# A two-layer transformer block on one core: routed rows without their gate row, an on-chip join at the end, new engine orders and no filler matmuls

## The chip, the cores and the metric

One core of a Trainium2 chip runs the kernel as a single program. The metric is device time in microseconds (us), the median over the runs shown. Beside it stands one profiled execution, whose trace gives the start and length of every instruction.

## What is computed

Eight sequences of 256 tokens, 256 wide, in float32, go through two layers. In each, a mixer and then a feed-forward part are added to `x` under gains `ga`, `gb` that depend on the sequence:

```python
x = x + ga * _L0_attn_ref(h, ...)     # causal attention, 16 heads, 4 kv heads
x = x + gb * _L0_ffn_ref(h, ...)      # 8 experts of width 176, top 2, and a shared one
x = x + ga * _L1_attn_ref(h, ...)     # linear attention with a memory
x = x + gb * _L1_ffn_ref(h, ...)      # 16 experts of width 256, top 4
# _L1_ffn_ref: G = gates of the top 4 (softmax), else 0
h = jnp.einsum('mh,eoh->emo', t, w1) + b1[:, None, :]
act = a * jax.nn.sigmoid(ALPHA * a) * (b + 1.0)
y = jnp.einsum('emi,edi->emd', act, w2) + b2[:, None, :]
return x + jnp.einsum('me,emd->md', G, y)
```

The change concerns the last part. Its 2048 tokens have four experts each, so 8192 (token, expert) pairs are computed, and each pair's result is scaled by its gate in `G` and by the sequence's gain row `gb` and summed into its token's row.

## The kernel before, in words

The work is cut into eight batches `b` of 256 tokens (one sequence each). For a batch, attention of layer 0 (128 units `u` of one head and one sequence, stages `scores`, `s_max`, `s_exp`, `p_t`, `pv`, `o_out`, `wo`), the first feed-forward part (`f_...`, `s_...`, `d_...`), linear attention of layer 1 (`qk_mm`, `vv_mm`, `ls_mm`, `num`, `o1`, `wo1`) and routing (`f_src` to `f_send`) follow each other, while attention of later batches goes on beside them. TensorE, VectorE (DVE), ScalarE (ACT), GpSimd (POOL) and the DMA queue of SyncE (SP) each run one fixed list of stages. `lay_out()` makes these lists before the program is built: it gives each stage a weight (`ENGINE`), a time to land (`LANDING`) and each chain of stages an allowance (`ALLOWED`, `DURING`, `BEHIND`), and always takes the chain that comes first by these numbers. An engine that waits holds up all that stands behind in its list.

**Routing.** Each batch's tokens are written to their experts' regions of a table `xsD` in DRAM. A row has `ROW` = 529 numbers: 256 of the token, its number, 16 gates and, from 273 on, the 256 numbers of the gain row `gb`, halved, which ACT puts there (`f_gb`, L1353). POOL sends the rows with eight indirect DMAs a batch (`f_send`, L1990), each of 128 rows. Earlier, SP fills the whole table with zero rows (`clear`, L820).

**Blocks.** When five batches are routed (`PART`), DVE and TensorE count the rows of each expert (`n_mm`, `n_blk`, `n_pre`, `n_tab`, `n_sel`, `n_bi`) and blocks of 128 rows begin: `FIRST` = 22 blocks from the first five batches, mixed with the rest of the other work, and then 57 more in a plain loop, 79 in all (`NBLK`). Block `n` is loaded by SP (`xb`, L851, into a ring `XB`), turned by TensorE (`x_t`, L1133), multiplied with its expert's `w1` in two halves (`h_m0`, `h_mm`, L1140), which ACT scales into `WS` (`w_in`, L1423) from `W1` (loaded in pieces by `w12`, L870, the last when the last `wo` is done), activated by DVE and ACT (`e_a` L1844, `e_tanh`, `e_b`, `e_g`, `e_act` L1864), and multiplied with `w2` (`y_mm`, L1161; `w2x`, L860). DVE multiplies the result by the gate and by the gain row (`y_out`, L1872) into one of five buffers `YB`, and POOL adds it by an indirect accumulating DMA to the tokens' rows in DRAM (`y_add`, L2019; the row numbers come from `tok`, L2009). Even blocks add to the output itself, odd ones to a second array `accD`. Two adds to one array never run together: `y_add(n)` waits for `y_add(n-2)`, and `y_out(n)` for `y_add(n-5)`, whose buffer it takes.

**Output.** POOL finishes a batch's `x` (`f_gain` L1977, `f_x` L1982), SP stores it to the output (`store`, L874), and the adds go on top. At the end one accumulating DMA adds `accD` to the output (`merge`, L2025).

**Fillers.** `FILL` names twelve stages of TensorE ahead of whose waits `fill` issues products of a constant (L900, 128x512, 35 in all) that nobody reads.

```python
def fill(*stage):
    n = FILL.get(stage, 0)
    ...
    for _ in range(n):
        pe.matmul(bank[plan.at[stage]][:, :], identb, cb16[:, 0:512], start=True, stop=True)
```

Of the kernel before, what the change touches and what calls it, by code (L numbers as in the profile page):

```python
# [15 lines left out]
NBLK, REG, ROW = 79, 2048 + 128, 529  # L16
# [3 lines left out]

PIECES, INSIDE = (range(0, 6), range(6, 11)), (range(0, 5), range(4, 8))
# [3 lines left out]
ALLOWED = {"keys": (0.04, 0.932), "query": (0, -0.52), "first": (0.1, 0.1), "shared": (0.04, 0.04), "dense": (0, -0.127), "linear": (0.08, 0.004), "late": (0.1, 0.201), "route": (0.1, 0.108), "gain": (0.1, 0.336), "count": (0.1, 0.207), "weights": (0.1, -0.153), "token": (0.2, 0.25), "unit": (0.1, 0.438), "block": (0.2, 0.2), "turn": (0.18, 0.044)}  # L25
DURING, BEHIND = {5: 0, 6: 0}, {5: -2.03, 6: 0.04, 7: 0}
# [4 lines left out]
    for name, stages in {  # L31
# [3 lines left out]
        "route_on_pe": "f_t f_gate f_rank s_mm s_t", "route_on_act": "f_sq f_src f_ht f_hb f_gb f_sig f_exp s_tanh s_at",  # L35
# [16 lines left out]
    for engine, stages in {  # L52
        "PE": "n_mm 0.25 n_pre 0.2 n_sel 0.95 x_t 0.25 h_m0 0.9 h_mm 1.07 y_mm 0.95 g_t 0.25 g_mm 0.95 h_t 0.45 k_mm 1.72 v_mm 1.72 k_t 0.45 mod_mm 1.72 modc_mm 3.6 f_t 0.47 f_gate 0.9 f_rank 0.4 s_mm 1.2 s_t 0.22 d_mm 0.3 d_t 0.42 d_y 2.15 "
              "p_t 0.33 scores 0.67 q_mm 1.73 q_t 0.45 pv 0.65 wo 0.87 qk_mm 1.73 vv_mm 0.84 ls_mm 0.65 num 0.56 o1_t 0.22 wo1 0.91",
        "ACT": "w_in 1.45 x_out 0.38 e_tanh 0.43 g_out 0.4 h_mod 1.05 k_sq 1.6 v_out 0.6 f_ht 0.62 f_hb 0.62 f_sig 0.2 f_sq 0.9 f_src 0.9 f_gb 0.6 f_exp 0.7 s_tanh 0.3 s_at 0.38 d_tanh 0.35 d_at 0.7 "
               "silu_t 0.3 gate_t 0.2 s_exp 0.99 p_tout 0.5 q_tout 0.62 p_norm 0.82 o_out 0.4 el_exp 0.64 vv_out 0.4 o1_out 0.4",
        "DVE": "n_blk 0.9 n_tab 1 n_bi 0.5 e_a 0.65 e_b 0.62 e_g 0.43 e_act 0.43 y_out 0.5 g_add 0.75 silu 0.4 b1_one 0.1 gate 0.2 zrow 0.13 ones_v 0.06 mod_out 0.7 mod_clamp 1.5 mod_one 0.3 modc_out 0.3 ln_var 1.25 ln_x 0.76 f_var 0.2 f_top 1.05 f_hot 0.75 f_gw 0.5 f_sum 0.3 f_macc 0.2 f_w 0.9 f_pos 0.95 "
# [127 lines left out]
def do(stage, *key, **how):  # L185
# [9 lines left out]
    ((("scores", NU - 1),), (11, 12), (15, 16)),  # L195
    ((("pv", NU - 1),), (13, 14)),
    ((("wo", NU - 1),), (9, 10)),
)


FILL = {
    ('num', 6, 0): 3,
    ('f_t', 0, 7): 6,
    ('h_m0', 0): 3,
    ('d_t', 7, 0, 1): 2,
    ('f_rank', 1, 6): 3,
    ('y_mm', 2): 2,
# [1875 lines left out]
```

## Time and profile before

| | |
|---|---|
| median of 3 runs | 1038.71 us (1037.44 to 1038.74) |
| profiled execution | 1032.54 us, its span 1030.5 us |
| instructions | 20559 |
| mean granted TensorE clock | 0.981 of full speed |
| TensorE busy | 976.0 us, 95% of the span |
| DVE, ACT, POOL busy | 716.3, 674.0, 427.2 us |

The page of the profile lists busy times by engine, the span in slices, the DMA queues and the costliest groups. PE is TensorE (its weight loads are PEld), SPq and POOLq are the queues of SP and POOL, and a line such as L1872 is a line of the kernel. The clock of TensorE is given as a share of 2.4 GHz. Time after `<-` says what ended the idle time before an instruction.

### The profile page before, as it was taken

What the parts mean: (1) busy time and instruction counts of PE and PEld (TensorE: products, weight loads), DVE (VectorE), ACT (ScalarE), POOL (GpSimd) and SP (SyncE); (2) the same over time, 40 slices, a digit from 0 to 9 for tenths busy, and PEclk for the clock granted to TensorE, in tenths of its full rate; (3) what the DMA queues carried; (4) which work ended last, traced back from release to release, by engine and by line L of the source; (5) the groups of instructions that cost most, each with busy time, mean ns of one, the idle gap of its engine ahead of it and who ended that gap; (6) DMA issues with size and microseconds to landing.
All of it is one profiled execution on the core that took longest, in us unless ns stands there. A gap on an engine that the chain in (4) does not pass through costs nothing. (4 is left out here: it accounts for less than half of the span.)

```text
span 1030.5 us, 20559 instructions
## 1 busy us (share of the span) xinstructions
PE 976.0 (95%) x6074; PEld 822.2 (80%) x6074; DVE 716.3 (70%) x2498; ACT 674.0 (65%) x1944; POOL 427.2 (41%) x447
## 2 busy tenths in 40 slices
PE   8999999999999999999999999998979899999980
PEld 4769878978878887888888788886758689999980
DVE  3564656766776778777768767864877678888870
ACT  2757877688668667758867867784735367777650
POOL 3322512331361254165146216331174555666662
PEclk9999999999999999999999999999999999999995
DMA  9926992998699120020021004355176799999944
GB/s 307 305 88 240 377 375 74 349 378 307 219 347 376 70 84 23 2 104 33 1 94 43 2 1 166 95 205 187 28 197 143 213 253 223 224 229 219 228 118 82
DMA packets 94108, 180.52 MB, mean 175 GB/s; under 512 B 9949, under 2 KB 29085, under 8 KB 93229
## 3 DMA queue, kind: packets, MB, share of 16 engines
q1 hardware_dynamic: 73899, 148.55, 43.6%
q0 software_dynamic: 18752, 30.30, 12.9%
q8 instruction: 48, 0.79, 0.3%
q14 instruction: 63, 0.52, 0.2%
q10 hardware_dynamic: 1346, 0.36, 0.2%
HBM read 77.71 MB, written 107.99 MB: 180 GB/s over the span
## 5 line engine op out<-in xcount | busy, mean ns | idle before, releaser
L1957 POOL TENSOR_TENSOR RB<-RB 128x512 f32<-128x512 f32 x64 | 67.0, 1047 | 262.1 <-DVE RB L1741 262.0
L1140 PE MATMUL bank<-RB 128*128 128x128 f32 x1264 | 157.3, 276 | 2.2 <-ACT RB L1423 0.8
L1140 PEld LDWEIGHTS bank<-RB 128*128 128x128 f32 x1264 | 149.6, 192 | 5.6 <-ACT RB L1423 1.8
L1106 PE MATMUL bank<-RA,RB 128*128 128x256 f32 x512 | 133.5, 383 | 4.8 <-ACT RB L1324 4.8
L1423 ACT ACTIVATE RB<-RA,nw 128x512 f32 x158 | 105.6, 716 | 43.0 <-issue 16.9
L1078 PE MATMUL bank<-RA 128*128 128x256 f32 x512 | 121.4, 380 | 1.6 <-DMA RA<-in_L_attn_Wq 1.6
L1078 PEld LDWEIGHTS bank<-RA 128*128 128x128 f32 x512 | 94.9, 190 | 17.0 <-issue 2.8
L1106 PEld LDWEIGHTS bank<-RA,RB 128*128 128x128 f32 x512 | 91.6, 191 | 18.5 <-ACT RB L1324 5.7
L1933 POOL TENSOR_TENSOR qs<-qs,half 128x4 f32<-128x4 f32 x64 | 65.7, 1026 | 62.7 <-DVE qs L1750 49.6
L1161 PE MATMUL bank<-RB,BC 128*128 128x256 f32 x316 | 83.8, 389 | 2.2 <-DVE BC L1864 1.3
L1324 ACT ACTIVATE RB<-bank 128x256 f32<-128x256 f32 x128 | 48.7, 381 | 52.0 <-PE bank L1097 47.0
L1741 DVE COPY RB<-bank 128x512 f32<-128x512 f32 x64 | 44.2, 691 | 49.0 <-PE bank L1078 48.7
L1990 POOL DMA_INDIRECT xsD<-SC,pu x64 | 65.1, 1018 | 31.1 <-DVE pu L1677 16.7
L1096 PE MATMUL bank<-RB,RA 128*128 128x256 f32 x256 | 77.4, 384 | 0.0
L1305 ACT ACTIVATE RB<-bank 128x384 f32<-128x384 f32 x128 | 62.0, 490 | 22.2 <-PE bank L1057 22.0
L1068 PE MATMUL bank<-RA 128*128 128x256 f32 x256 | 76.4, 380 | 0.0
L1298 ACT ACTIVATE RB<-RB,sm 128x128 f32<-128x128 f32 x128 | 50.8, 397 | 24.0 <-DVE sm L1762 19.6
L1318 ACT ACTIVATE RB<-RB,sm 128x256 f32<-128x256 f32 x128 | 64.0, 500 | 0.0
L1299 ACT ACTIVATE RB<-RB,sm 128x256 f32<-128x256 f32 x128 | 63.9, 499 | 0.0
L1057 PE MATMUL bank<-ident,RB 128*128 128x128 f32 x384 | 63.2, 274 | 0.0
L1161 PEld LDWEIGHTS bank<-RB,BC 128*128 128x128 f32 x316 | 55.2, 194 | 9.7 <-DVE BC L1864 2.4
L1844 DVE TENSOR_SCALAR RB<-bank,b 128x128 f32<-128x128 f32 x158 | 48.1, 346 | 21.1 <-PE bank L1140 14.4
(255 smaller groups left out, 2381.8 us busy)
## 6 DMA issues: line engine op xcount, KB each, us to landing
xsD<-BC SPq DMA_DIRECT2D x17, 4232.0 KB, 32.9
RB<-in_w2b SPq DMA_DIRECT2D x79, 256.0 KB
RB<-xsD SPq DMA_DIRECT2D x61, 264.5 KB, 3.6
BC<-modD SPq DMA_DIRECT2D x16, 512.0 KB, 4.2
RA<-in_w SPq DMA_DIRECT2D x10, 512.0 KB
X<-xsD SPq DMA_DIRECT2D x18, 264.5 KB, 3.0
RA<-in_L_attn_Wq SPq DMA_DIRECT2D x1, 2048.0 KB, 13.8
RA<-in_L_attn_Wo SPq DMA_DIRECT2D x1, 2048.0 KB, 19.7
```

The lines of the kernel that those rows point to most:

```text
L1068: pe.matmul(ps[:, 128:384], q[:, 128:256], k[:, 0:256], start=True, stop=True).then_inc(mine("scores", u), 1)
L1078: m = pe.matmul(psum("q_mm", p)[:, t * 256:t * 256 + 256], hT[:, b % 2, c, t * 128:t * 128 + 128], Wq[:, c, h * 128:h * 128 + 256], start= ...
L1096: pe.matmul(psum("pv", u)[:, 0:256], v[:, 0, :], PT[:, u % 2, 0:256], start=True, stop=False, skip_group_check=True)
L1106: m = pe.matmul(bank[5][:, t * 256:t * 256 + 256], OT[:, u % 2, t * 128:t * 128 + 128], Wo[:, h, :], start=(h == 0 and t == 0), stop=(h == ...
L1140: m = pe.matmul(ps[:, 128 * j:128 * j + 128], WS[:, n % 2, c, 128 * j:128 * j + 128], XT[:, n % 2, c * 128:c * 128 + 128], start=(c == 0), ...
L1161: m = pe.matmul(ps[:, 0:256], AB[:, n % 3, c * 128:c * 128 + 128], W2[:, n % 4, c, :], start=(c == 0), stop=(c == 1))
L1299: act.activation(P[:, u % 4, 128:384], P[:, u % 4, 128:384], ACT.Exp, bias=s[:, 3:4], scale=-1.0, accum_out=s[:, 5:6]).then_inc(mine("s_ex ...
L1318: act.activation(P[:, u % 4, 128:384], P[:, u % 4, 128:384], ACT.Copy, scale=s[:, 7:8]).then_inc(mine("p_norm", u), 1)
L1423: m = act.activation(WS[:, n % 2, c, :], W1[:, bass.ds(r, 1), c, :].rearrange("p a n -> p (a n)"), ACT.Copy, scale=nw[:, c:c + 1])
L1933: pool.tensor_tensor(dst, src, half[:, 0:n], ALU.pow).then_inc(sem, 1)
L1957: pool.tensor_tensor(sq, qrow, qrow, ALU.mult).then_inc(mine("q_sq", p), 1)
L1990: pool.indirect_dma_start(xsD[:, :], bass.IndirectOffsetOnAxis(pu[:, i, k:k + 1], 0), route(1)["src"][:, i, 0:ROW], None).then_inc(mine("f ...
```

## The change

- Rows of `xsD` shrink from 529 to 273 numbers: the gain row is gone from `clear`, `f_send` and `xb`, with the stage `f_gb` that wrote it. `y_out` multiplies by the gate and 0.5 alone.
- All adds go to two arrays of their own, `accA` and `accB`, both set to zero early on. `store` and `merge` are gone. After the last add SP loads `accA` (`sum_a`) and ACT's queue `accB` (`sum_b`), 256 KB each for a batch; `join` adds the two, multiplies by the gain rows (`gains`, loaded in the loop) and adds `x`, for batches 2 and 5 on POOL and for the others on DVE; `put` stores the batch.
- Blocks' ring buffers `XB` and `YB` move: blocks 1 to 4 load only after the last `q_t` and after `s_x(6, 1)`.
- The numbers of the plan are others, so every engine's order is new, and `FILL` is empty.

```diff
-NBLK, REG, ROW = 79, 2048 + 128, 529
+NBLK, REG, ROW = 79, 2048 + 128, 273
...
+JOIN_POOL = 2, 5
...
-FILL = {
-    ('num', 6, 0): 3,
-    ('f_t', 0, 7): 6,
-    ('h_m0', 0): 3,
...
+FILL = {}
...
-DURING, BEHIND = {5: 0, 6: 0}, {5: -2.03, 6: 0.04, 7: 0}
+DURING, BEHIND = {5: 0, 6: -0.09, 7: -2.38}, {5: -1.78, 6: -0.2, 7: 0}
...
-        after = [("n_bi", 0), ("store", PART - 1), ("f_send", 1, PART - 1, 1, 3)] + [("q_t", NU // 2 - 1)] * (n == RINGS[0] - 1) + [("y_out", n - RINGS[0]), ("tok", n - RINGS[0])] * (n >= RINGS[0])
+        after = [("n_bi", 0), ("f_send", 1, PART - 1, 1, 3)] + [("q_t", NU // 2 - 1)] * (n == 1) + [("s_x", NB - 2, 1)] * (1 < n < RINGS[0]) + [("y_out", n - RINGS[0]), ("tok", n - RINGS[0])] * (n >= RINGS[0])
...
-    p.add("merge", by=16)
+        if n == lo + 16:
+            p.add("gains", by=16)
+    for b in range(NB):
+        p.add("sum_a", b, slot=b, by=16)
+        p.add("sum_b", b, slot=b, by=16)
+    for b in range(NB):
+        p.add("join", b, slot=b in JOIN_POOL)
+        p.add("put", b, by=16)
...
-        accD = nc.dram_tensor("accD", (2048, 256), F32, kind="Internal").ap()
+        accA, accB = (nc.dram_tensor(f"acc{i}", (2048, 256), F32, kind="Internal").ap() for i in "AB")
...
+            def gains_in():
+                on.wait_ge(*done("s_x", NB - 1, 1))
+                sp.dma_start(gains, modD[1][:, 1280:1536].unsqueeze(0).broadcast_to([128, 8, 256])).then_inc(mine("gains"), 16)
+
+            def sum_a(b):
+                on.wait_ge(*done("w_in", NBLK - 1))
+                on.wait_ge(*done("y_add", NBLK - 1 - NBLK % 2))
+                on.wait_ge(*done("y_add", NBLK - 2 + NBLK % 2))
+                sp.dma_start(sumA[:, 2 * b:2 * b + 2, :], acc_v[0][:, 2 * b:2 * b + 2, :]).then_inc(mine("sum_a", b), 16)
+
+            def put(b):
+                on.wait_ge(*done("join", b))
+                sp.dma_start(out_v[:, b, :, :], sumA[:, 2 * b:2 * b + 2, :]).then_inc(mine("put", b), 16)
...
-                act.activation(route(1)["src"][:, :, 273:529], row(1, b, 768), ACT.Copy, scale=0.5).then_inc(mine("f_gb", b), 1)
...
+            def sum_b(b):
+                on.wait_ge(*done("w_in", NBLK - 1))
+                for n in (NBLK - 2, NBLK - 1):
+                    on.wait_ge(*done("y_add", n))
+                act.dma_start(sumB[:, 2 * b:2 * b + 2, :], acc_v[1][:, 2 * b:2 * b + 2, :]).then_inc(mine("sum_b", b), 16)
...
-                dve.scalar_tensor_tensor(YB[n % 5], psum("y_out", n)[:, 0:256], rows(n)[:, bass.ds(ex[n] + 257, 1)], rows(n)[:, 273:529], ALU.mult, ALU.mult).then_inc(mine("y_out", n), 1)
+                dve.tensor_scalar(YB[n % 5], psum("y_out", n)[:, 0:256], rows(n)[:, bass.ds(ex[n] + 257, 1)], 0.5, ALU.mult, ALU.mult).then_inc(mine("y_out", n), 1)
...
+            def join(b):
+                if (b in JOIN_POOL) != False:
+                    return
+                t, x = sumA[:, 2 * b:2 * b + 2, :], X[:, 2 * b:2 * b + 2, :]
+                on.wait_ge(*done("sum_a", b))
+                on.wait_ge(*done("sum_b", b))
+                dve.tensor_tensor(t, t, sumB[:, 2 * b:2 * b + 2, :], ALU.add).then_inc(ch.sem, ch.up())
+                on.wait_ge(*done("gains"))
+                on.wait_ge(ch.sem, ch.n)
+                dve.tensor_tensor(t, t, gains[:, b:b + 1, :].broadcast_to([128, 2, 256]), ALU.mult).then_inc(ch.sem, ch.up())
+                on.wait_ge(ch.sem, ch.n)
+                on.wait_ge(*done("f_x", b))
+                dve.tensor_tensor(t, t, x, ALU.add).then_inc(mine("join", b), 1)
...
-                on.wait_ge(*done("store", (PART if n < FIRST else NB) - 1))
...
-                pool.indirect_dma_start((out_r, accD)[n % 2], bass.IndirectOffsetOnAxis(to[:, n % 6:n % 6 + 1], 0), YB[n % 5], None,
+                pool.indirect_dma_start((accA, accB)[n % 2], bass.IndirectOffsetOnAxis(to[:, n % 6:n % 6 + 1], 0), YB[n % 5], None,
...
-                pool.dma_start(out_r.rearrange("(a c) n -> a (c n)", c=8), accD.rearrange("(a c) n -> a (c n)", c=8),
-                               accum_op=ALU.add, max_dma_last_dim=8192).then_inc(mine("merge"), 16)
```

`join` on POOL has the same three operations for batches 2 and 5.

**Place 1: POOL, where the block adds begin.** L1990 and L2003 are `f_send` before and after, L2019 and L2031 `y_add`, L2009 and L2022 `tok`, L1933 and L1947 a small square-root step. Before, the eight sends of batch 6 stand behind the adds of blocks 1 and 2 and ahead of that of block 3:

```order
L2019 DMA accD<-BC,to 2048x256 [waits tok_0,block_on_dve_0]
L2009 COPY to<-X 128x1 [waits y_add_0,xb_1]
L2019 DMA out<-BC,to 2048x256 [waits tok_0,block_on_dve_0]
L1990 DMA xsD<-SC,pu 34944x529 [waits clear_12,clear_13,route_on_act_0,route_on_dve_0]
L1990 DMA xsD<-SC,pu 34944x529
L1933 TENSOR_TENSOR rs<-rs,half 128x2 [waits norm_on_dve_0]
L1990 DMA xsD<-SC,pu 34944x529 x6
L2019 DMA accD<-RB,to 2048x256 [waits y_add_1,tok_0,block_on_dve_0]
```

After, they stand ahead of the first add:

```order
L2022 COPY to<-BC 128x1 [waits xb_2]
L1947 TENSOR_TENSOR rt<-rt,half 128x2 [waits route_on_dve_0]
L2022 COPY to<-BC 128x1 [waits xb_3]
L2022 COPY to<-BC 128x1 [waits xb_4]
L2003 DMA xsD<-SC,pu 34944x273 [waits clear_13,clear_12,route_on_dve_0]
L2003 DMA xsD<-SC,pu 34944x273 x7
L2031 DMA accA<-BC,to 2048x256 [waits acc_zero_0,tok_0,block_on_dve_0]
L2031 DMA accB<-BC,to 2048x256 [waits tok_0,block_on_dve_0]
```

So no add is behind that burst once the adds have begun, and all five `YB` buffers can fill before the first add goes out. The sends of batch 7 stand ahead of the add of block 13 before, and of block 14 after.

**Place 2: TensorE, from the last `wo` (L1106, L1107) to the first block product.** L1205 and L1206 are `ls_mm`, L900 the fillers, L1214 to L1219 `num`, L971 `f_t`. Before:

```order
L1106 MATMUL bank<-RA,RB 128x256
L1205 MATMUL bank<-SC 128x256 [waits lin_on_dve_0]
L1206 MATMUL bank<-SC 128x128
L900 MATMUL bank<-cb 128x512 [waits lin_on_act_0]
L900 MATMUL bank<-cb 128x512 x2
L1214 MATMUL bank<-Mz,SC 128x129 [waits lin_on_dve_0]
L1216 MATMUL bank<-SC 128x129
L1214 MATMUL bank<-Mz,SC 128x129
L1218 MATMUL bank<-SC 128x129
L1219 MATMUL bank<-SC 128x129
L900 MATMUL bank<-cb 128x512 x6
L971 MATMUL bank<-ident,SC 128x128 [waits f_add_1]
```

After (L1134 is `x_t`, L1228 `o1_t`, L1236 `wo1`, L972 `f_t`, L1010 `s_mm`, L1141 the first block product):

```order
L1107 MATMUL bank<-RA,RB 128x256
L1134 MATMUL bank<-ident,SC 128x128 [waits xb_0,s_max_0]
L1134 MATMUL bank<-ident,SC 128x128
L1228 MATMUL bank<-ident,SC 128x128 [waits lin_on_dve_0]
L1228 MATMUL bank<-ident,SC 128x128
L1134 MATMUL bank<-ident,RB 128x128 [waits xb_1,block_on_act_0]
L1134 MATMUL bank<-ident,RB 128x128
L1236 MATMUL bank<-RB,SC 128x256 [waits lin_on_act_0,b2_on_dve_0]
L1236 MATMUL bank<-RB,SC 128x256
L972 MATMUL bank<-ident,SC 128x128 [waits f_add_1]
L972 MATMUL bank<-ident,SC 128x128 x3
L1010 MATMUL bank<-RB,SC 128x360 [waits route_on_act_0]
```

`ls_mm` and `num` of batch 6 have moved ahead of the last `wo`, and the turns of blocks 0 and 1 behind it. The count of the first five batches (`n_mm` to `n_sel`) has moved too: in the trace of before it stands at 615 to 628 us, and in the new order its last step stands 14 rows ahead of the last `wo`.

**Place 3: SP, at the end.** Before, its list ends with loads of `w2`, and POOL's `merge` is the last transfer. After, behind the last load of `w2`:

```order
L872 DMA RA<-accA 128x2x256 [waits y_add_0,y_add_1,block_on_act_0]
L872 DMA RA<-accA 128x2x256 x7
L876 DMA out<-RA 128x2x256 [waits join_False] x2
L876 DMA out<-RA 128x2x256 [waits join_True]
L876 DMA out<-RA 128x2x256 [waits join_False] x2
L876 DMA out<-RA 128x2x256 [waits join_True]
L876 DMA out<-RA 128x2x256 [waits join_False] x2
```

The loads wait for the last adds to both arrays, and each store for its batch's join.

## Rows read from the trace of the kernel before

**Rows 1.** The page: busy time by engine

```profile
PE 976.0 (95%) x6074; PEld 822.2 (80%) x6074; DVE 716.3 (70%) x2498; ACT 674.0 (65%) x1944; POOL 427.2 (41%) x447
```

**Rows 2.** Stretches: us, busy PE, PEld, DVE, ACT, POOL; clock, DMA share, GB/s

```profile
600.00:650.00 50.00, 50.00 (x320) 44.19 (x318) 36.22 (x142) 33.55 (x101) 24.87 (x24) 1.00 0.27 96
...
709.00:829.00 120.00, 104.70 (x688) 83.84 (x687) 90.31 (x314) 60.87 (x143) 53.89 (x56) 0.96 0.57 151
829.00:1003.00 174.00, 172.22 (x1302) 161.40 (x1300) 141.59 (x420) 117.71 (x234) 106.52 (x118) 1.00 0.88 215
```

**Rows 3.** Short stretches between 690 and 830, the same columns

```profile
694.00:696.00 2.00, 0.27 (x2) 0.00 (x0) 0.50 (x2) 0.00 (x0) 1.31 (x2) 1.00 0.95 382
...
762.00:764.00 2.00, 2.00 (x14) 1.83 (x13) 0.00 (x0) 0.00 (x0) 1.50 (x2) 1.00 0.91 331
...
768.00:770.00 2.00, 0.01 (x1) 0.00 (x0) 0.34 (x1) 0.00 (x0) 2.00 (x4) 1.00 0.99 221
```

**Rows 4.** TensorE by time: start us, us, what, [idle before, and its end]

```profile
697.33 1.82 PE L1106 MATMUL bank<-RA,RB 128*128 128x256 f32 x4 [3.06 <-ACT RB L1324]
...
701.18 1.03 PE L1106 MATMUL bank<-RA,RB 128*128 128x256 f32 x4
...
710.48 0.81 PE L900 MATMUL bank<-cb 128*128 128x512 bf16 x3
...
716.37 2.05 PE L1140 MATMUL bank<-RB 128*128 128x128 f32 x16 [0.40 <-ACT RB L1423]
...
771.60 1.25 PE L900 MATMUL bank<-cb 128*128 128x512 bf16 x5 [3.58 <-DVE BC L1872]
...
817.07 1.89 PE L900 MATMUL bank<-cb 128*128 128x512 bf16 x4 [3.14 <-issue]
```

**Rows 5.** POOL by time, two sends of batch 6

```profile
760.92 0.96 POOL L1990 DMA_INDIRECT xsD<-SC,pu  x1 [0.30 <-DVE RB L1844]
762.19 0.96 POOL L1990 DMA_INDIRECT xsD<-SC,pu  x1 [0.30 <-issue]
```

**Rows 6.** ACT's group of f_gb: busy us, mean ns | idle before

```profile
L1353 ACT ACTIVATE SC<-BC 128x512 f32<-128x512 f32 x8 | 5.0, 624 | 0.0
```

**Rows 7.** POOL and DVE by time at the end

```profile
999.87 1.56 POOL L2019 DMA_INDIRECT accD<-RB,to  x1 [1.53 <-DMA out<-BC,to]
...
1003.04 0.48 DVE L1872 SCALAR_TENSOR_TENSOR RB<-bank,RB 128x256 f32<-128x256 f32 x1 [0.56 <-DMA accD<-RB,to]
...
1007.66 1.56 POOL L2019 DMA_INDIRECT accD<-BC,to  x1 [0.16 <-issue]
1009.53 1.55 POOL L2019 DMA_INDIRECT out<-RB,to  x1 [0.30 <-issue]
1012.83 1.05 POOL L2025 DMA_DIRECT2D out<-accD  x1 [1.75 <-DMA out<-RB,to]
```

**Rows 8.** DMA issues: count, KB each, median us from issue to landing

```profile
out<-accD POOLq DMA_DIRECT2D x1, 2048.0 KB, 13.1
X<-xsD SPq DMA_DIRECT2D x5, 264.5 KB, 3.0
```

**Rows 9.** Stretches with full queues: merge, loads from DRAM twice, stores to it

```profile
1019.00:1022.00 3.00, 0.00 (x0) 0.00 (x0) 0.00 (x0) 0.00 (x0) 0.00 (x0) 0.50 1.05 218
...
20.00:30.00 10.00, 8.42 (x43) 6.24 (x43) 6.51 (x22) 5.01 (x16) 6.41 (x7) 1.00 1.11 347
30.00:40.00 10.00, 10.00 (x55) 8.13 (x54) 5.84 (x24) 8.26 (x26) 3.62 (x4) 1.00 1.02 292
...
86.00:120.00 34.00, 34.00 (x201) 30.60 (x200) 20.77 (x78) 25.01 (x79) 12.15 (x12) 1.00 1.04 365
```

**Rows 10.** An add of 128x512 on DVE and on POOL: busy us, mean ns

```profile
L1780 DVE TENSOR_TENSOR X<-X,SC 128x512 f32<-128x512 f32 x2 | 1.4, 692 | 0.1
...
L1982 POOL TENSOR_TENSOR X<-X,SC 128x512 f32<-128x512 f32 x8 | 9.3, 1168 | 0.5
```

## Prediction before the run

> **What bounds the kernel now.** I read first the busy times [rows 1], then stretches of the span, to see where TensorE is not busy. From 50 to 690 us it is busy throughout at its full clock, as in the stretch shown [rows 2]: whatever DVE, ACT, POOL or a DMA does faster there is worth nothing by itself. From 829 to 1003 us, the plain loop of blocks, it is busy for 172.2 of 174 us [rows 2]: the loop too is TensorE's. What is left to win lies in two places. One is the stretch from 690 to 829 us, where TensorE stands for 120 - 104.7 = 15.3 us after 709 [rows 2] and for 3.06 us before it [rows 4], works for a while at half clock and carries the fillers. The other is the end, 1030.5 - 1003 = 27.5 us with no matmul in it.
>
> In the first place I looked for the longest waits. Three are of 3.1 to 3.6 us [rows 4]: at 694, 768 and 814 us. In and around all three DVE and ACT stand as well, while POOL sends rows and the DMA engines are busy for 91 to 99% of the time [rows 3]. At 762 us neither DVE nor ACT runs anything for 2 us although TensorE goes on. The sends go out every 762.19 - 760.92 = 1.27 us [rows 5], each with 128 rows of 2116 bytes, 271 KB: 213 GB/s from this one source. That is the load which the change halves.
>
> At the end, the last `y_out` starts at 1003.04, but its add goes out at 1009.53 only; POOL has fallen behind, because each add waits for the one two before it to land (at 999.87 it stood 1.53 us for that). The merge starts at 1012.83 [rows 7] and lands 13.1 us later [rows 8], at 1025.9; 4.6 us remain to the end of the span.
>
> **The change part by part.** I sum against the profiled execution's 1032.54 us, which is 6.2 us (0.6%) under the median, and carry the difference over.
>
> *Fillers.* Three take 0.81 us and five 1.25 us [rows 4], so one costs 0.22 us and 35 cost 7.7 us. Twelve of them (3 + 6 + 3, the first at 710.48) stand between the last `wo` and the first block product at 716.37 [rows 4], which waits for the last piece of `W1` and for ACT, not for them. These 2.6 us come back as waiting. Of the other 23, 5.1 us, some stand in waits too; those at 817.07 begin after the wait and are all cost. I take -4.0; the bounds are 0 and -7.7.
>
> *Shorter rows, the waits.* `f_send`, `xb` and `clear` carry 52% of their bytes (273 of 529 numbers). A burst of eight sends then asks for 110 GB/s in place of 213. If the three waits of 3.06, 3.58 and 3.14 us hang on that load, 9.8 us of waiting go, and the half clock after them: the four products of L1106 took 1.82 us after the wait and 1.03 later [rows 4], and I put 1.2 us to each of three, so 13.4 us in all. If they hang on the number of transfers, which stays, nothing goes. Nothing in the trace tells these apart; I take about half, -7.0, with 0 and -13.4 as bounds.
>
> *Shorter rows, the rest.* `f_gb` takes 8 x 0.62 = 5.0 us off ACT [rows 6], beside a TensorE that is always busy. `clear` writes half as much, between 85 and 320 us, where nobody waits for it. Both count 0. If that cover were gone, `f_gb` would give its 5.0 us, no more. `y_out` multiplies one row less; in the loop DVE is busy for 141.6 of 174 us [rows 2], so this is 0 too. The second zeroing is a store of 2 MB at about 55 us that no stage waits for before the first add; 0.
>
> *New orders.* DVE has 90.3 us of work in the 120 us from 709 [rows 2], TensorE 104.7 with the fillers in. So both could be packed tighter by some us. For it speaks that the sends of batch 6 now stand ahead of the first add and not between the adds of blocks 2 and 3. Against it speaks that the count of the first five batches, long done before, now ends 14 rows ahead of the last `wo`. Behind it hang DVE's table, SP's table load and a block load that takes 3.0 us to land [rows 8], and TensorE's first turn waits for it directly behind the last `wo`. What is queued behind is the linear attention and `s_mm`, which have until the last piece of `W1` comes anyway: the first block product started 5.9 us after the first filler behind the last `wo` (710.48 to 716.37) [rows 4]. `ls_mm` and `num`, moved ahead of the last `wo` where TensorE is full, cost 0.8 us there and give it back behind. I take -2.0 for this part, within +4 and -7. The attention stretch before 690 us has no idle time to lose and can only get worse; I take +0.5, up to +3.
>
> *The adds at the end.* A block now moves 140 + 262 + 131 KB and not 271 + 262 + 131 KB, 20% less, so an add should land earlier and POOL fall less behind. Were it not behind at all, the adds of blocks 76, 77 and 78 would go out at the pace of the last two, 1.87 us [rows 7], from about 1003, the last at 1006.8 and not at 1009.5. I take -2.0 of these 2.7 us, bounds 0 and -3.5.
>
> *The join for the merge.* The merge moves 2.1 MB at 218 GB/s [rows 9]. In its place stand 4.19 MB of loads and 2.10 MB of stores. Loads from DRAM with all queues full ran at 347 GB/s, and at 292 in another stretch; stores to DRAM at 365 [rows 9]: 12.1 + 5.7 = 17.8 us. A lone load of 264.5 KB lands after 3.0 us [rows 8], of which 0.8 is its bytes at 347 GB/s, so 2.2 us stand ahead of the first bytes and about as much behind the last: 22.2 us. Stretches at up to 382 GB/s [rows 3] would make it 16.5 + 4.4 = 20.9. A join is three operations of 0.69 us on DVE [rows 10], six batches 12.5 us, and 1.17 us each on POOL, two batches 7.0 us; both run while the loads come in. The last batch's join (2.1 us) and its store stand beside the backlog of stores, so they add nothing. I take 21.5 us against the merge's 13.1: +8.4, between +6 and +11.4.
>
> The Trainium skill ("DMA: Bandwidth & Descriptors", Anatomy of one DMA) fits one large transfer as about 2.0 us and its bytes at 436 GB/s. By it the loads and the stores would be 9.6 + 4.8 + 2 x 2.0 = 18.4 us, and this term +5.3; no stretch of this trace with large loads shows that rate for long.
>
> Sum: -4.0 - 7.0 - 2.0 + 0.5 - 2.0 + 8.4 = -6.1 us for the profiled execution, 1026.4 us. On the median that would be 1032.6; since the largest gain is the least certain one and the largest loss the surest, I round up to **1033.5 us**. About 2 us (0.2%) is what a measurement of this kernel can tell from no change.
>
> **The rivals.**
>
> *A, the forecast:* the middle gives 10 to 15 us, the end costs 4 to 8. 1029 to 1036.5 us. Chance 0.36.
>
> *B, the middle closes well:* all three long waits and the half clock go, the fillers give 5 and the orders 4, and the end costs 6.4: -5 - 13.4 - 4 + 0.5 - 2 + 6.4 = -17.5, about 1021 us, from 1017 to 1029. For it speaks that all three waits fall in times with 91 to 99% DMA share [rows 3]; against it that the loop runs at 88% without them [rows 2]. Chance 0.17.
>
> *C, nothing moves:* the waits depend on the count of transfers, not on bytes. Then -4 - 3 + 0.5 - 2 + 8.4 = -0.1: 1038.6 us, from 1036.6 to 1040.8. Chance 0.15.
>
> *D, the burst ahead of the first add, slower:* this rival has one place, POOL ahead of `y_add(0)`. Eight sends hold it for 8 x 1.27 = 10.2 us [rows 5]. There are five buffers `YB`; if `y_mm` of block 5 is ready before the first add has landed, DVE stops at `y_out(5)`, and with it everything that DVE does for the other chains. If all of the 10.2 us reach TensorE, the sum is -6.1 + 10.2 = +4.1, 1042.8 us. It decides from 6.1 us on, and from 8.1 us the kernel is measurably slower. With the end at its upper bound it is 3 us more. Against it speaks that dense work of batch 7 stands beside the first blocks. Chance 0.18.
>
> *E, the clock falls where fillers held it up, slower:* the wait of 710 to 716 us and about five short ones had products in them; without them TensorE is idle there. After each of the three long waits the granted clock was low, at 1.2 GHz against 2.4, and L1106 took 1.82 us against 1.03 [rows 4]. Six such falls at 1.2 to 1.6 us are 7.2 to 9.6 us, the sum +1.1 to +3.5: 1039.8 to 1042.2,. Chance 0.14. The Trainium skill ("TensorE: Matmul & The Clock Gate", The HAM clock gate) says that the array is throttled by default and only sustained activity releases it; by that rule the fillers bought clock. The trace agrees as to the fall after the long waits, and cannot show what happens without fillers.
>
> **How the numbers follow.** Faster is A nearly whole, B, and a piece of C: 0.36 + 0.17 + 0.01 = 0.54. The same is most of C and a little of E: 0.16. Slower is the rest of D and E: 0.30. For eight times in ten I leave out the lower part of B and the upper end of D and E: 1021 to 1046 us. A's own range is 1029 to 1036.5.
>
> **What would show it.** The shorter rows: between 690 and 830 us no stretch in which DVE and ACT both stand while POOL sends. Rival E: a granted clock under 0.9 in slices where the trace of before has 1.00. Rival D: DVE at `y_out` waiting for an add among the first six blocks. The end: from the landing of the last add to the end of the span 24 to 29 us, where before it was 17.7; and the last add less than 5 us behind the last `y_out`. I am wrong if attention itself, up to the last `wo`, is more than 3 us longer, or if the plain loop, 174 us before, is not as long.

## The result and the profile after

The changed kernel takes **1042.72 us** (1040.58 to 1045.67, 12 runs), the kernel before 1035.58 us beside it; the ratio is **1.0066** (95% interval 1.005 to 1.0083). It is slower by some 7 us. Two repeats gave 1.0082 (1.0058 to 1.0106) and 1.0085 (1.0066 to 1.0104). The direction is the opposite of the forecast. The range, 1021 to 1046 us, held the number, and with some luck: it was set around a kernel before of 1038.71 us, which took 1035.58 here; by the ratio the forecast's own base would have given 1045.6.

The busy times of the page after, against [rows 1]:

```profile
PE 974.1 (94%) x6039; PEld 824.6 (79%) x6039; DVE 731.5 (70%) x2516; ACT 671.1 (64%) x1936; POOL 433.3 (42%) x452
```

The stretches of [rows 2], of the kernel after, and then 740 to 760 us:

```profile
600.00:650.00 50.00, 49.96 (x317) 43.96 (x316) 38.34 (x142) 34.03 (x106) 22.30 (x23) 1.00 0.19 66
709.00:829.00 120.00, 96.79 (x626) 80.42 (x627) 89.04 (x303) 60.99 (x142) 55.30 (x63) 0.89 0.48 120
829.00:1003.00 174.00, 173.17 (x1301) 162.65 (x1301) 139.50 (x413) 117.61 (x234) 105.88 (x116) 0.99 0.79 178
740.00:760.00 20.00, 15.19 (x71) 10.64 (x70) 11.48 (x35) 6.55 (x17) 9.87 (x11) 0.69 0.41 107
```

Attention is as full as before, and the plain loop is as long: from its first `y_out`, that of block 22, to the last one it takes 164.0 us before (839.00 to 1003.04) and after (843.97 to 1008.00). What is lost in the middle is lost between 690 us and the start of the loop. From 709 to 829 us the queues carry 120 GB/s and no longer 151, but TensorE is busy for 7.9 us less and its granted clock is 0.89 against 0.96 [rows 2]. From 740 to 760 us, with waits of TensorE in it, the clock is 0.69; the same 20 us of before:

```profile
740.00:760.00 20.00, 18.99 (x145) 15.62 (x143) 18.01 (x67) 11.64 (x29) 7.89 (x8) 1.00 0.40 101
```

Where the waits are, by DVE, ACT and then TensorE in time, kernel after (the long waits of before are in [rows 4]):

```profile
697.99 0.15 DVE L1790 TENSOR_SCALAR spi<-bank 16x1 int32<-16x1 f32 x1 [4.28 <-remote]
745.45 0.42 DVE L1689 TENSOR_TENSOR SC<-bank,BC 128x256 f32<-128x256 f32 x1 [2.56 <-remote]
821.44 0.48 DVE L1872 TENSOR_SCALAR BC<-bank,SC 128x256 f32<-128x256 f32 x1 [4.65 <-remote]
...
745.49 0.41 ACT L1377 ACTIVATE SC<-bank,gh 128x176 f32<-128x176 f32 x1 [4.21 <-remote]
```

```profile
746.44 0.47 PE L1028 MATMUL bank<-RB,SC 128*128 128x352 bf16 x2 [1.73 <-issue]
751.06 0.77 PE L1028 MATMUL bank<-RB,SC 128*128 128x352 bf16 x2 [2.28 <-DVE SC L1636]
823.21 2.04 PE L1162 MATMUL bank<-RB,BC 128*128 128x256 f32 x4 [5.48 <-DVE BC L1864]
```

"Remote" is the profile's word where it finds no releaser. Each of these DVE and ACT instructions reads a PSUM bank (the on-chip memory that TensorE writes) whose product, by the rows, had ended some 2 to 6 us before: they stand for a product of TensorE that reaches them late. I call these the late products. All fall in bursts of eight sends or within 2 us behind one; that of batch 6 goes from 736.87 to 746.88 us. The four products at 823.21 then take 2.04 us, at half clock.

The end, POOL, SP and DVE in time (before: [rows 7]):

```profile
1012.55 1.54 POOL L2031 DMA_INDIRECT accA<-RB,to  x1 [0.30 <-issue]
1023.25 1.26 POOL L2040 TENSOR_TENSOR RA<-RA 128x512 f32<-128x512 f32 x1 [9.16 <-DMA RA<-accB]
...
1030.99 1.59 POOL L2046 TENSOR_TENSOR RA<-RA,X 128x512 f32<-128x512 f32 x1
```

```profile
1015.35 4.27 SPq L872 DMA_DIRECT2D RA<-accA  x8
```

```profile
1008.00 0.48 DVE L1872 TENSOR_SCALAR RB<-bank,RB 128x256 f32<-128x256 f32 x1 [0.57 <-issue]
1018.90 0.69 DVE L1921 TENSOR_TENSOR RA<-RA 128x512 f32<-128x512 f32 x1 [10.41 <-DMA RA<-accB]
...
1029.72 1.74 DVE L1921 TENSOR_TENSOR RA<-RA 128x512 f32<-128x512 f32 x1
1031.50 1.63 DVE L1924 TENSOR_TENSOR RA<-RA,SC 128x512 f32<-128x512 f32 x1
1033.16 0.69 DVE L1927 TENSOR_TENSOR RA<-RA,X 128x512 f32<-128x512 f32 x1
...
1037.27 0.69 DVE L1927 TENSOR_TENSOR RA<-RA,X 128x512 f32<-128x512 f32 x1
```

The last add goes out 4.55 us behind the last `y_out` (before 6.49). The loads begin at 1015.35 and the span ends at 1040.5: 25.15 us, against 17.7 from the merge's start. DVE's join operations take 0.69 us each until POOL's begin, then 1.63 to 1.74, and 0.69 again once POOL is done.

### The profile page after: what moved, and what is told of

Read it like the earlier page. It is cut to its first block and busy times, and to the rows that moved or that the text cites. A ratio compares the mean times of both kernels' runs of the same rounds, so it can differ in the third digit from the quotient of the medians.

```text
span 1040.5 us, 20534 instructions
## 1 busy us (share of the span) xinstructions
PE 974.1 (94%) x6039; PEld 824.6 (79%) x6039; DVE 731.5 (70%) x2516; ACT 671.1 (64%) x1936; POOL 433.3 (42%) x452
## 5 line engine op out<-in xcount | busy, mean ns | idle before, releaser
L1141 PE MATMUL bank<-RB 128*128 128x128 f32 x1264 | 159.9, 278 | 3.4 <-ACT RB L1417 1.6
L1141 PEld LDWEIGHTS bank<-RB 128*128 128x128 f32 x1264 | 151.9, 194 | 6.0 <-ACT RB L1424 1.9
L1107 PE MATMUL bank<-RA,RB 128*128 128x256 f32 x512 | 133.8, 384 | 1.0 <-ACT RB L1325 1.0
L1107 PEld LDWEIGHTS bank<-RA,RB 128*128 128x128 f32 x512 | 92.4, 192 | 15.3 <-issue 3.5
L1947 POOL TENSOR_TENSOR qs<-qs,half 128x4 f32<-128x4 f32 x64 | 66.1, 1032 | 91.0 <-DVE qs L1750 78.2
L2003 POOL DMA_INDIRECT xsD<-SC,pu x64 | 64.7, 1011 | 35.5 <-DVE pu L1677 21.8
L1761 DVE CUSTOM_DVE_ANT_0 RB<-bank,cb,qs 128x128 f32<-128x128 f32 x128 | 44.4, 347 | 37.8 <-PE bank L1069 35.0
L1377 ACT ACTIVATE SC<-bank,gh 128x176 f32<-128x176 f32 x128 | 48.9, 405 | 26.5 <-PE bank L1028 18.8
```

What stands on the lines that cost most here:

```text
L1107: m = pe.matmul(bank[5][:, t * 256:t * 256 + 256], OT[:, u % 2, t * 128:t * 128 + 128], Wo[:, h, :], start=(h == 0 and t == 0), stop=(h == ...
L1141: m = pe.matmul(ps[:, 128 * j:128 * j + 128], WS[:, n % 2, c, 128 * j:128 * j + 128], XT[:, n % 2, c * 128:c * 128 + 128], start=(c == 0), ...
L1947: pool.tensor_tensor(dst, src, half[:, 0:n], ALU.pow).then_inc(sem, 1)
L2003: pool.indirect_dma_start(xsD[:, :], bass.IndirectOffsetOnAxis(pu[:, i, k:k + 1], 0), route(1)["src"][:, i, 0:ROW], None).then_inc(mine("f ...
```

## The experiments

The sets ran on five chips. The kernel before took 1035 to 1037 us beside e1 to e4, f1 to f4 (both sets on one chip), h1, h2 and i1 (a chip each), and 1023 to 1024 us beside e5 to e8 (one chip) and g2 to g4 (another). So I call them "late" and "prompt" chips, and compare ratios within a set. The kernel before beside itself came out at 0.9982 (f1), so a ratio within 0.2% of 1 says little by itself.

Six of the kernels leave something out, for time alone: e4 the gain, e5, f4, g2 and g3 the rows of batches 5 to 7, e8 the joins. One more, g1, was to space the sends in another way; its buffer did not fit into SBUF, so it has no time.

| run | what | us | ratio to before (95%) | chip |
|---|---|---|---|---|
| e1 | after, plan's numbers of before | 1037.01 | 1.0019 (1.001 to 1.0029) | late |
| e2 | e1 with fillers | 1039.56 | 1.0033 (1.0019 to 1.0047) | late |
| e3 | before, no fillers | 1037.24 | 1.0019 (1.0007 to 1.0031) | late |
| e4 | before, short rows | 1031.46 | 0.9964 (0.9951 to 0.9976) | late |
| e5 | before, tiny sends | 1015.33 | 0.9915 (0.989 to 0.9939) | prompt |
| e6 | before, spaced sends | 1027.47 | 1.0042 (1.0028 to 1.0056) | prompt |
| e7 | e1, joins on DVE | 1021.29 | 0.997 (0.9955 to 0.9985) | prompt |
| e8 | e1, no join operations | 1019.02 | 0.9949 (0.9931 to 0.9967) | prompt |
| f1 | before, again | 1033.61 | 0.9982 (0.9964 to 0.9999) | late |
| f2 | after, again | 1044.4 | 1.0082 (1.0058 to 1.0106) | late |
| f3 | after, joins on DVE | 1041.29 | 1.0052 (1.0028 to 1.0076) | late |
| f4 | as e5 | 1015.61 | 0.9807 (0.9775 to 0.9838) | late |
| g2 | before, plain sends | 1023.01 | 0.9982 (0.9969 to 0.9995) | prompt |
| g3 | after, tiny sends | 1020.37 | 0.9967 (0.9952 to 0.9981) | prompt |
| g4 | as e7 | 1019.85 | 0.997 (0.9956 to 0.9985) | prompt |
| h1 | as e6 | 1028.63 | 0.9942 (0.9919 to 0.9965) | late |
| h2 | after, again | 1043.07 | 1.0085 (1.0066 to 1.0104) | late |
| i1 | combined | 1027.76 | 0.9908 (0.9893 to 0.9924) | late |

### The parts of the change: e1 to e4

e1 takes the changed kernel and gives the plan its old numbers (`ALLOWED`, `DURING`, `BEHIND`, the weights and landing times); e2 also brings `FILL` back.

```diff
-DURING, BEHIND = {5: 0, 6: -0.09, 7: -2.38}, {5: -1.78, 6: -0.2, 7: 0}
+DURING, BEHIND = {5: 0, 6: 0}, {5: -2.03, 6: 0.04, 7: 0}
```

> The changed kernel, with the plan's numbers (allowances, weights, landing times) of the kernel before; rows, join, buffers and the empty list of fillers stay as changed. Theory O (the new orders cost about 4 to 5 of the 10 us that the profiled execution grew by): 4 to 5 us under the changed kernel, about 1038. Theory T (orders are worth nothing, the tail costs 5 us and the middle lost what the fillers' removal should have given): within 2 us of the changed kernel, 1041 to 1045. If the orders of before are worse for the new buffers: above 1045.

> As e1_old_numbers, and with the twelve groups of fillers of the kernel before, at the same stages. If the fillers hold the clock up (rival E): 2 to 8 us faster than e1_old_numbers. If they are pure cost: 2 to 7.7 us slower. If they stand in waits: the same within 1.5 us.

e3 is the kernel before with `FILL = {}`:

> The kernel before with the list of fillers empty, nothing else touched, so that its order is the same. The forecast's term says 4 us faster (0 to 7.7) than before: 1031.5. Rival E says 1 to 4 us slower, with a lower granted clock between 700 and 830 us. If waits simply take their place: the same within 1 us.

e4 is the kernel before with two lines of the change:

```diff
-NBLK, REG, ROW = 79, 2048 + 128, 529
+NBLK, REG, ROW = 79, 2048 + 128, 273
...
-                dve.scalar_tensor_tensor(YB[n % 5], psum("y_out", n)[:, 0:256], rows(n)[:, bass.ds(ex[n] + 257, 1)], rows(n)[:, 273:529], ALU.mult, ALU.mult)
+                dve.tensor_scalar(YB[n % 5], psum("y_out", n)[:, 0:256], rows(n)[:, bass.ds(ex[n] + 257, 1)], 0.5, ALU.mult, ALU.mult)
```

> The kernel before with rows of 273 numbers in the table, its clears, sends and block loads, and the result multiplied by the gate and 0.5 alone, so the gain is left out of the output; orders, fillers, f_gb and merge are as before. Theory bytes (the three long waits hang on the load of the sends): 7 to 13 us faster than before, about 1026, and no wait of over 2 us on TensorE between 690 and 830 us. Theory count (they hang on the number or the row of sends): within 2 us of before, with waits of 3 us still at the ends of the bursts.

The new numbers cost 1.0066 - 1.0019, about 5 us (theory O), and up to 6.8 us by the two repeats. Taking the fillers out of the kernel before did not give the 4 us of the forecast: e3 is 1.9 us slower, which is no more than f1 differs from the same kernel beside it, and in e1's order they cost 1.4 to 2.5 us. From 709 to 829 us e3 shows

```profile
709.00:829.00 120.00, 97.11 (x622) 81.84 (x623) 87.37 (x304) 59.47 (x141) 50.84 (x53) 0.91 0.54 142
```

so TensorE is busy for 7.6 us less, nearly the whole price of the 35 products, but at a clock of 0.91 and not 0.96 (f1, the kernel before again: 0.93). The fall lies where twelve fillers stood, from 710 to 720 us; before and then e3:

```profile
710.00:720.00 10.00, 8.91 (x52) 6.03 (x52) 7.29 (x24) 4.44 (x8) 0.72 (x1) 1.00 0.56 195
710.00:720.00 10.00, 6.15 (x33) 5.14 (x32) 6.78 (x21) 3.52 (x6) 0.72 (x1) 0.78 0.63 205
```

The short rows alone are 3.9 us faster, between the ranges of both theories, and all long waits are still there; DVE and TensorE of e4 in time:

```profile
695.08 0.42 DVE L1689 TENSOR_TENSOR SC<-bank,BC 128x256 f32<-128x256 f32 x1 [3.44 <-remote]
763.49 0.48 DVE L1872 TENSOR_SCALAR X<-bank,RB 128x256 f32<-128x256 f32 x1 [2.65 <-remote]
769.08 0.69 DVE L1881 TENSOR_SCALAR SC<-bank 128x512 f32<-128x512 f32 x1 [3.40 <-remote]
816.97 0.48 DVE L1872 TENSOR_SCALAR X<-bank,RB 128x256 f32<-128x256 f32 x1 [3.35 <-remote]
```

```profile
696.93 2.08 PE L1106 MATMUL bank<-RA,RB 128*128 128x256 f32 x4 [2.94 <-ACT RB L1324]
771.03 1.50 PE L900 MATMUL bank<-cb 128*128 128x512 bf16 x5 [3.57 <-DVE BC L1872]
```

Half the bytes leave the first two waits of [rows 4] at 2.94 and 3.57 us (before 3.06 and 3.58), and DVE's at 816.97 at 3.35. Theory bytes falls.

### What makes the waits: e5, e6, f1, f4, g2, h1

In e5 and f4 each send of batches 5 to 7 is a store of one number. In g2 it is a plain store of the same 128 rows to one block of DRAM. In e6 and h1 a small operation of POOL stands ahead of each send, which is otherwise as it was. The edit of e5 and f4, and that of e6 and h1:

```diff
+                if b >= 5:
+                    pool.dma_start(tinyD[8 * b + 4 * i + k:8 * b + 4 * i + k + 1, 0:1], route(1)["src"][0:1, i, 0:1]).then_inc(mine("f_send", l, b, i, k), 16)
+                    return
```

```diff
+                if b >= 5:
+                    c = 8 * (b - 5) + 4 * i + k
+                    pool.tensor_tensor(pad[:, c:c + 1], half[:, 0:1], half[:, 0:1], ALU.pow)
                 pool.indirect_dma_start(xsD[:, :], ...
```

> The kernel before, but the 24 sends of batches 5 to 7 are plain stores of one number to a small table of their own, issued by POOL at the same places with the same semaphores; those batches' rows are missing from the output, and blocks that held them add less. Theory sends (the long waits after 690 us come from the indirect sends themselves, by their count of row descriptors): no wait of DVE or ACT over 1.2 us on a finished product in 690 to 830 us, and 8 to 14 us faster. Theory program (they lie in the order of the list or in other loads, and only coincide with the sends): waits of about 3 us at the same lines, L1689, L1872, L1881, L1872, and less than 4 us gained.

> The kernel before, with one small power operation of POOL ahead of each of the 24 sends of batches 5 to 7, so that they go out every 2.0 to 2.3 us instead of every 1.27. Theory rate (the queue of sends in flight makes the waits): the waits of 3 us go or fall under 1.5 us, and the time is within 3 us of before, since POOL's adds start some 8 us later. Theory count or program: the waits stay at 3 us or more, and the kernel is 0 to 5 us slower.

Neither e5 nor e6 has such a wait, but nor have e7 and e8, which send as ever: this chip has none, and e5 and e6 could tell nothing of their cause. (e7 differs from e1 in the joins at the end alone, and e1, on a late chip, has DVE waits of 2.13 and 4.46 us at 814 and 824 us.) The sets f and h asked again.

> The kernel before, unchanged, profiled on the chip of this set of runs. In the set of e5 to e8 the kernel before took 1022.98 us against 1035.35 in the set of e1 to e4, and no kernel of that set shows a DVE or ACT wait over 1.2 us on a finished product after 690 us. Theory chip (those waits are the chip's, not the kernel's): if before is about 1023 us here, its trace has none of them; if it is about 1035, it has all four (3.5, 2.7, 3.4 and 3.3 us). Theory kernel (only the edits of e5 to e8 took them away): they are there at either time.

> The kernel of e5 once more: the 24 sends of batches 5 to 7 are stores of one number. On a chip whose f1 shows the long waits, theory sends: none of them over 1.2 us, and 8 to 20 us faster than before; theory program or loads: they stay, less than 8 us gained. On a chip without them: 7 to 8 us faster, as in e5, which is then the price of the sends and of the adds left out alone.

> The kernel of e6, with sends of batches 5 to 7 every 1.85 us. If the kernel before takes about 1035 us beside it: theory pace says at most 3 us of wait in sum at the four lines and 5 to 9 us faster than before, theory count says waits of 2.5 us or more each and 2 to 5 us slower. If before takes about 1023: 4 us slower, as in e6.

> The kernel before, but the 24 sends of batches 5 to 7 go, with the same 128 rows of 2116 bytes each, as plain stores into a block of a table of their own; their rows are missing from the output. Theory indirect (looking up 128 row numbers each makes the waits): as f4, no wait, and 1014 to 1018 us. Theory rows (any store of 128 row pieces at this pace from POOL's queue): the four waits stay, and the time is 7 to 9 us under before, as the missing adds alone gave in e5.

DVE's waits in f1, the kernel before on a late chip:

```profile
695.45 0.42 DVE L1689 TENSOR_TENSOR SC<-bank,BC 128x256 f32<-128x256 f32 x1 [3.65 <-remote]
764.84 0.48 DVE L1872 SCALAR_TENSOR_TENSOR X<-bank,RB 128x256 f32<-128x256 f32 x1 [1.93 <-remote]
770.47 0.69 DVE L1881 TENSOR_SCALAR SC<-bank 128x512 f32<-128x512 f32 x1 [3.44 <-remote]
819.71 0.48 DVE L1872 SCALAR_TENSOR_TENSOR X<-bank,RB 128x256 f32<-128x256 f32 x1 [3.35 <-remote]
```

The first of them in f4 (L1690 is this line there):

```profile
692.47 0.42 DVE L1690 TENSOR_TENSOR SC<-bank,BC 128x256 f32<-128x256 f32 x1 [0.35 <-PE bank L1051]
```

and in h1, with its sends by POOL:

```profile
693.81 0.42 DVE L1690 TENSOR_TENSOR SC<-bank,BC 128x256 f32<-128x256 f32 x1 [0.35 <-PE bank L1051]
...
690.45 1.05 POOL L1994 DMA_INDIRECT xsD<-SC,pu  x1 [0.18 <-issue]
691.53 0.57 POOL L1993 TENSOR_TENSOR pad<-half 128x1 f32<-128x1 f32 x1
692.29 1.04 POOL L1994 DMA_INDIRECT xsD<-SC,pu  x1 [0.19 <-issue]
```

The same instruction, with the same producer, waits 3.65 us in f1 and 0.35 us in f4 and in h1, and no "remote" wait of DVE or ACT over 1.2 us is left in either between 680 and 840 us. f4 is 20 us faster than before, where e5, the same kernel on a prompt chip, gains 7.7: f4 and e5 both take 1015 us, so the late chips lose some 12 us, and only through these sends and what hangs on them. h1 keeps every send and byte and widens the step from 1.27 to 1.84 us: 7 us faster on a late chip, 4.5 slower on a prompt one (e6), 1027 to 1029 us on both. Theory pace holds; whether it is the gap or the operation in it that helps, no run separates. The kernel before agrees in its earlier batches, which it sends at a slower pace and which show no such wait. The eight sends of batch 0 take 33 us from the first to the last, and those of batch 4 come 1.3 to 2.3 us apart, 12 us in all, with never more than three on the quick step. In batches 5 to 7 six or more follow each other at 1.26 to 1.46 us. The second and third send of batch 0:

```profile
273.40 1.00 POOL L1990 DMA_INDIRECT xsD<-SC,pu  x1 [0.30 <-issue]
281.21 1.04 POOL L1990 DMA_INDIRECT xsD<-SC,pu  x1 [0.20 <-issue]
```

g2 fell on a prompt chip and can't tell whether being indirect matters, and it also changed the pace: seven of its stores go out within 3.90 us. It met neither of its forecasts. Its ratio is 0.7% above that of e5, about 7 us, and a block load for which TensorE waits 5.17 us at 809 us is a part of that.

### Whether the new orders cost by themselves: f2, h2, g3

> The changed kernel, unchanged, beside f1. If the loss is of the orders and the tail, its ratio to before is 1.005 to 1.009 on this chip too. If the loss comes through the long waits of the middle, and this chip has none, the ratio falls to 1.002 or less.

> The changed kernel, unchanged. In g3, where nothing waited for sends, its last product ended 3 us before that of e5 (985.5 against 988.7 us), and its end took 33.1 us against 25.5. If before takes about 1023 us beside it, theory waits (the new orders lose only through the long waits) says a ratio of 0.999 to 1.004; theory order (they lose by themselves) says 1.005 to 1.008. If before takes about 1035: 1.006 to 1.009, as before.

> The changed kernel with the sends of batches 5 to 7 as in f4; their rows are missing from the output. f4 took 1015.6 us. Theory order (the new numbers and the lack of fillers cost by themselves): 5 us or more over f4, so 1020 to 1026. Theory waits (the new orders only put the waits where they hurt more, 3 to 5 us of the loss): at most 2 to 4 us over f4, 1017 to 1019.5, of which 3 us are the join on POOL.

f2 and h2 both fell on late chips and only repeat the result. g3, at 1020.37 us, lies in the range of theory order (1020 to 1026) and above that of theory waits (to 1019.5). Its trace says where the time goes. The last products of e5 and of g3, by TensorE in time:

```profile
987.58 1.10 PE L1162 MATMUL bank<-RB,BC 128*128 128x256 f32 x4 [0.83 <-DVE BC L1865]
```

```profile
984.36 1.10 PE L1163 MATMUL bank<-RB,BC 128*128 128x256 f32 x4 [0.83 <-DVE BC L1865]
```

With the sends out of the way the changed kernel ends its products 3.2 us earlier, 985.5 against 988.7; it is 5 us slower in the whole because its end takes 1018.6 - 985.5 = 33.1 us against 1014.2 - 988.7 = 25.5. With the sends in, on late chips, it ends them later: at 1007.4 to 1009.3 in its three traces, against 1002.9 and 1006.8 in the two of before. So what comes before the end loses time, 0.6 to 6.4 us by these traces, only where the products are late. That compares the whole change up to there, shorter rows and missing fillers included, and for g3 and e5 it rests on one trace each, on two chips.

It doesn't say that the new numbers are free. By ratios, g3 is 1.0052 of e5 (0.9967 against 0.9915). Its join on POOL is about 0.3% of that (f3 against f2), so 0.2% is left. The old numbers, with the join on DVE, stand at 0.997 of before (e7, g4). If tiny sends gave that kernel what they gave the kernel before on such a chip, 0.85%, the new numbers would cost about 0.5% there too, as they do on late chips. This is an estimate from sums of ratios, and short sends may gain less by being taken out. The old numbers with tiny sends were not run, nor was the changed kernel as it stands on a prompt chip. So whether the new orders lose through late products or by themselves stays open.

### The end: e7, e8, f3, g4

f3, e7 and g4 set `JOIN_POOL = ()`. e8 copies one column in place of the three operations.

> e1_old_numbers with all eight batches joined on DVE and none on POOL. Theory shared port (DVE's join operations took 1.63 to 1.74 us beside POOL's against 0.69 alone): eight batches at 2.1 us are 16.6 us, the tail is 2 to 3 us shorter than in e1_old_numbers, about 1034.5. If loads bound the tail: the same as e1_old_numbers. If DVE bounds it without any slowdown by POOL: 2 to 4 us slower than e1_old_numbers.

> e1_old_numbers with a copy of one column in place of each batch's three join operations, all on DVE; the output holds the first array's sums alone. It shows what the loads and stores of the end cost without compute. If the DMA bounds the tail: within 1.5 us of e7_old_numbers_dve_join. If DVE bounds it: 3 to 6 us faster than e1_old_numbers, about 1032.5.

> The changed kernel with all batches joined on DVE. Theory shared port: 2 to 3 us faster than f2. If it is only the loads: the same within 1 us. If eight joins on one engine bound the end: 1 to 4 us slower.

> e7 once more. On a chip with the waits, from e1's 1.0019 and 3 us less for the join on DVE: ratio 0.998 to 1.001. If the old numbers' gain on the other chip was from the lack of waits alone, above 1.002.

f3 is 3.1 us faster than f2. From its first load, at 1015.86, to its end at 1038.8 are 22.9 us, all 24 operations at 0.68 to 0.69 us; in e8 the same piece is 996.97 to 1018.0, 21.0 us:

```profile
996.97 4.12 SPq L872 DMA_DIRECT2D RA<-accA  x8
1001.13 11.98 SPq L876 DMA_DIRECT2D out<-RA  x8
```

So transfers alone are 21.0 us to the end of the span, the joins on one engine add 1.9 (in e7, of e8's own set, 1.6), and POOL's help costs 2.2 more. The rows show DVE slowed by more than a factor of two, 0.69 to 1.74 us, while POOL works too, and POOL by less: 1.26 to 1.59 us against a lone 1.17 [rows 10]. Both read pairs of SBUF tiles. The Trainium skill ("SBUF — State Buffer", Who interferes with whom) says that a DVE instruction with two SBUF inputs and a GpSimd instruction that reads SBUF take turns on one shared pair of ports; the rows agree, with 0.69 us against 1.63 to 1.74.

### All together: i1

The changed kernel with the plan's numbers of before, joins on DVE and spaced sends.

> The changed kernel with the plan's numbers of before, all batches joined on DVE, and a small power operation of POOL ahead of each of the 24 sends of batches 5 to 7. From g4 (1019.9 us, no long waits) and 4.5 us for the pace (e6 over before): 1024 to 1025 us on any chip. Beside a before of about 1035 us the ratio is 0.988 to 0.992, beside one of about 1023 it is 1.000 to 1.002. If the pace of the shorter sends is still too fast for a chip with waits: 1028 or more.

1027.76 us beside 1036.95: 0.9% faster than before on a late chip, with no "remote" wait over 1.2 us. The ratio is in its range, the time is 3 us over the 1024 to 1025 that I expected. The changed kernel was not run beside it; on other late chips it took 1042.7 to 1044.4. Spacing has a price in i1's trace: at 824.74 us a `y_out` waits 3.79 us for an add that the slower sends had held up. On a prompt chip i1 was not run; g4, the same without the spacing, took 1019.85 there.

## Why the prediction was wrong, step by step

**The steps that failed are "Shorter rows, the waits" and "New orders".** Against the forecast of -6.1 us the result was about +7, a gap of 13. The new orders are 7 of it and the shorter rows 5, since e4 brings 3.9 us for both of their terms and not 9.0. The fillers account for the rest.

**"Shorter rows, the waits", -7.0, was 0.** I read 91 to 99% DMA share beside the waits [rows 3], priced them by bytes and took half of 13.4 us. Half the bytes leave the waits as they are (e4); the pace of the sends makes them (h1), and the change leaves that at 1.27 us. Rival C had this mechanism and too little chance; "the count" was also inexact, since h1 keeps the count.

**"New orders", -2.0 with +4 as its bound, was +5** (e1 against the changed kernel; 5 to 7 with the repeats). I summed idle time and work as if the new lists would meet the old waits. They meet others: ACT's of 4.21 us at 745 and DVE's of 4.65 at 821, each in front of work that TensorE needs. That these make the +5 is argued and not shown; g3 allows that a part of it comes without any late product.

**Fillers, -4.0, were +1.9 in the order of before** (e3) **and -1.4 to -2.5 in that of e1.** Neither is far from the 0.2% by which a kernel differs from itself, and nobody ran the new numbers with fillers, so how much of the +7 is theirs stays open. Rival E's mechanism is there, at 710 to 720 us: a granted clock of 0.78 without fillers (e3) against 1.00 with them, and 0.66 (e1) against 0.83 (e2). The Trainium skill ("TensorE: Matmul & The Clock Gate", The HAM clock gate), cited in the prediction, had this direction right. But the lowest stretch of the changed kernel, 0.69 from 740 to 760 us, is no proof of it. It stands behind waits of TensorE of 1.73 and 2.28 us, and the same stretch is low without fillers (e1) and with all of them (e2):

```profile
740.00:760.00 20.00, 16.19 (x86) 12.70 (x86) 13.55 (x38) 7.62 (x17) 12.10 (x12) 0.76 0.29 83
740.00:760.00 20.00, 15.06 (x83) 11.02 (x84) 11.91 (x37) 6.96 (x18) 10.32 (x11) 0.78 0.27 83
```

On prompt chips, with no late product and no filler, it is 1.00 (g4) and 0.91 (g3). The sign that I had named for rival E was thus seen, but it does not tell missing fillers from new waits.

**The adds at the end, -2.0:** the last add's lag fell by 6.49 - 4.55 = 1.9 us. Right: in e4, with short rows alone, it is 4.34 us and in f1 6.64. This is the likely home of at least half of e4's 3.9 us; its profile's end is 2.4 us shorter than that of before, its last products no earlier (1004.0 against 1002.9 us). (In the repeat f2 the lag was 5.70 us, in h2 4.56, so the sign "under 5 us" is a loose one.)

**The join, +8.4:** 25.15 - 17.7 = 7.5 us from the last adds' landing. Right in size by luck, since two errors cancel. My 21.5 us went to the landing of the last store, with the 4.6 us of before behind it, so 26.1 to the end of the span; transfers alone take 21.0 (e8), 5.1 less. In e8 next to nothing moves after 1016.4 us and the span ends at 1018.0, where before the last bytes move at 1025.0 and the span ends at 1030.5. The joins, put at nothing, cost 4.1.

**The attention stretch, +0.5,** has no loss up to 690 us: TensorE is busy for 638.8 of the 640 us from 50 on, before 638.4. **Rival D** did not come: no `y_out` among the first six blocks waits for an add. Of the signs I had named, the one for the shorter rows failed, that for E was seen, that for D was not, and both of the end were right (25.15 us, 4.55 us).

The parts add up, which speaks for them. Short rows -3.9, the join +7.5 and the fillers' absence in e1's order -1.4 to -2.5 give +1.1 to +2.2 us, and e1, which holds these and the moved buffers, measured +1.9. With the new numbers' +5 that is the result.

What stays open: by which path a burst of sends makes a finished product late, and why on some chips alone; whether indirect sends differ from plain ones; whether the new orders lose through the late products or by themselves; and how the changed kernel itself stands to before on a prompt chip, where it was not run.

## What to carry to other kernels

A wait that stands beside full queues isn't yet a wait for bytes: halve the bytes alone and look whether it shrinks, and change the pace alone. New orders meet other stalls than those of the old profile, so a price worked out from the old ones can have the wrong sign, as here. When two engines share a small job at the end, look whether their operations keep their lone durations; here one engine did it sooner than two.

## What the hardware showed that I had not expected

- The same kernel takes 1023 to 1024 us on some chips and 1035 to 1037 on others, and the difference lies in products that DVE and ACT see 2 to 6 us late while POOL sends 128 rows every 1.27 us. At 1.84 us it is gone. The Trainium skill ("SBUF — State Buffer", Who interferes with whom) says that a DMA never contends with a compute engine; the late products come with nothing but the sends' pace, so either that has an exception here, or the signal and not the data is late, or the cause lies elsewhere. No run tells which.
- Two traces of the same kernel can differ by more than a small change: the one of before shows 1032.54 us, f1's 1038.72, and the waits stand at the same four DVE lines in both. f1, the same kernel, also came out at a ratio of 0.9982 (0.9964 to 0.9999) to itself. Sums made from one trace are good to about 3 us here, ratios to 0.2%.
- Products that nobody reads can be worth their time: 7.6 us of them out, and nothing won (e3; 1.9 us lost, at the edge of the noise).
